# First layer of a two-layer cross-attention kernel: up projection as three fp32r products, keys and statistics at other positions

## The reference, cut to what matters

```python
q  = layer_norm(transpose(x   + pos_enc), ln_q_g,  ln_q_b)     # per batch: 512 tokens x 256 channels
kv = layer_norm(transpose(ctx + pos_enc), ln_kv_g, ln_kv_b)
Q, K, V = split(q @ Wq), split(kv @ Wk), split(kv @ Wv)         # 16 heads of 16
ctx = softmax(Q K^T / 4) V
r = ctx @ Wo + q
h = layer_norm(r, ffn_ln_g, ffn_ln_b)
h = gelu(h @ W1 + b1) @ W2 + b2                                 # 256 -> 512 -> 256
out = transpose(h + r)
```

## Time and profile before

| what | us |
|---|---|
| median of 3 runs | 1813.23 (1811.85 to 1816.99) |
| the profiled execution, its time | 1816.33 |
| its span, first to last instruction | 1814.5 |
| busy: PE, DVE, ACT, POOL | 1697.7, 1225.3, 1065.0, 166.1 |
| mean granted clock of TensorE | 0.96 |

### The profile page before, as it was taken

One profiled execution on the slowest core, in us unless ns is written; L12 is line 12 of the kernel. 1 busy time (PEld: TensorE's weight loads), 2 busy tenths in 40 slices (PEclk: granted clock), 3 DMA queues, 4 the chain that ended last, 5 costly groups with the idle time before them and its releaser, 6 DMA issues.

```text
span 1814.5 us, 32853 instructions
## 1 busy us (share of the span) xinstructions
PE 1697.7 (94%) x11968; PEld 1242.2 (68%) x11968; DVE 1225.3 (68%) x2812; ACT 1065.0 (59%) x2337; POOL 166.1 (9%) x221
## 2 busy tenths in 40 slices
PE   4779999999999998999999999999998799999999
PEld 3324444443534335788899888888887689999998
DVE  6667786867766653588888888888888653333332
ACT  3346666766666564587888777877778531111111
POOL 2102111010200000000000000000000100000000
PEclk7779999999999889999999999999999899999999
DMA  5322233222222224466567767666666330000000
GB/s 164 121 86 68 88 95 101 84 81 92 73 83 66 72 62 145 118 156 169 152 167 195 202 171 198 181 169 169 175 180 176 106 123 24 24 24 24 24 24 12
DMA packets 169481, 201.64 MB, mean 111 GB/s; under 512 B 25957, under 2 KB 117221, under 8 KB 169321
## 3 DMA queue, kind: packets, MB, share of 16 engines
q1 hardware_dynamic: 169032, 199.14, 38.8%
q10 hardware_dynamic: 288, 0.39, 0.1%
HBM read 131.84 MB, written 67.63 MB: 110 GB/s over the span
## 4 chain that ended last, share of the span: by engine, by line
PE 79%; DVE 12%; ACT 4%; issue 2%; DVEq 1%; DMA 0%; POOL 0%; ACTq 0%; SPq 0%
PE c_d L2230 10%; PE c_sums L2245 10%; PE b_d L1471 9%; PE b_d L1484 8%; PE a_d L531 5%; PE a_escore L504 5%; PE b_d L1551 5%; PE a_d L612 4%; PE a_d L620 3%; PE a_mscore L516 3%; DVE a_mx L870 3%; PE b_score L1539 3%; PE b_d L1568 3%; DVE b_t L1887 2%; DVE b_t L1883 2%
## 5 line engine op out<-in xcount | busy, mean ns | idle before, releaser
L870 DVE TENSOR_REDUCE a_mx<-a_mscore 128x2 f32<-128x1024 f32 x249 | 304.4, 1223 | 114.2 <-PE a_mscore L516 112.0
L689 ACT ACTIVATE a_pt<-a_escore 128x1024 f32<-128x1024 f32 x256 | 262.1, 1024 | 157.2 <-PE a_escore L504 156.6
L1709 ACT ACTIVATE b_pr<-b_t,b_nmax 128x256 f32<-128x256 f32 x512 | 254.5, 501 | 121.7 <-DVE b_nmax L1887 121.3
L2329 ACT ACTIVATE c_gT<-c_d,c_b 128x256 f32<-128x256 f32 x128 | 53.9, 473 | 266.9 <-PE c_d L2230 266.9
L1887 DVE CUSTOM_DVE_ANT_0 b_t<-b_t,b_minus 128x256 f32<-128x256 f32 x512 | 191.2, 429 | 16.9
L1883 DVE TENSOR_TENSOR b_t<-b_score,b_mask 128x1024 f32<-128x1024 f32 x128 | 155.1, 1212 | 64.3 <-PE b_score L1539 64.0
L2374 DVE CAST c_g_high<-c_gT 128x512 fp32r<-128x512 f32 x64 | 40.2, 627 | 172.0 <-ACT c_gT L2329 172.0
L504 PE MATMUL a_escore<-a_qst,a_kst 50*128 50x512 f32 x512 | 133.1, 516 | 18.4 <-ACT a_pt L689 16.8
L504 PEld LDWEIGHTS a_escore<-a_qst,a_kst 50*128 50x128 f32 x512 | 49.7, 191 | 143.7 <-ACT a_pt L689 87.8
L2230 PE MATMUL c_d<-c_ln_high,c_w_high 128*128 128x256 f32 x512 | 145.4, 284 | 2.4 <-DVE c_ln_low L2376 2.4
L2230 PE MATMUL c_d<-c_ln_low,c_w_high 128*128 128x256 f32 x512 | 145.6, 284 | 0.0
(11 more groups left out here) (175 smaller groups left out, 3301.2 us busy)
## 6 DMA issues: line engine op xcount, KB each, us to landing
b_qst<-b_q SPq DMA_DIRECT2D x96, 256.0 KB, 4.6
b_kst<-b_k SPq DMA_DIRECT2D x96, 256.0 KB, 6.4
b_q<-b_qparts SPq DMA_DIRECT2D x64, 256.0 KB, 4.0
b_k<-b_kparts SPq DMA_DIRECT2D x64, 256.0 KB, 3.5
a_qst<-a_q_parts SPq DMA_DIRECT2D x192, 64.0 KB, 2.2
a_kst<-a_k_parts SPq DMA_DIRECT2D x186, 64.0 KB, 2.2
a_q_parts<-a_qparts SPq DMA_DIRECT2D x32, 256.0 KB, 2.3
a_k_parts<-a_kparts SPq DMA_DIRECT2D x32, 256.0 KB, 2.4
```

The source lines that it names most:

```text
L689: nc.scalar.activation(pt[:, at % RING, :, :], escore[:], ACT.Exp, scale=SCALE).then_inc(exp_done.sem, 1)
L870: nc.vector.tensor_reduce(mx[:, 2 * pair:2 * pair + 2, q], maxima_bank(b, n)[:], AX_X, ALU.max).then_inc(max_done.sem, 1)
L1709: last = nc.scalar.activation(pr[:, u % 2, j, :], t[:, u % 2, j, :], ACT.Exp, scale=-1.0, bias=nmax[:, u, j:j + 1], accum_out=esum[:, u, j ...
```

## The change

The up projection `up` uses three fp32r products per step in place of one fp32 matmul. W1 gets a high and a low part (it is loaded to the staging area and split in iteration -1). Its input hT now lies in the third token tile, and its high and low parts (`high_hidden` on ScalarE, `low_hidden` on VectorE) in `pair`, the tile that also takes the parts of the context (`ctxp` before). The keys' second half moves from position 9 to 6 on all engines, the turn to channels of the network's input to slot 0 of position 5, both statistics of batch i+2 from positions 6 and 7 to 8 and their normalisations to 10 and 11 (but for iteration -2). The last quarter's `keep_up` moves to position 8.

```diff
@@ -129,7 +129,7 @@
         wo = sb("wo", [P, 2, CT, C], F32R)
-        w1 = sb("w1", [P, CT, F])
+        w1 = sb("w1", [P, 2, CT, F], F32R)
@@ -147,8 +147,7 @@
         ctxt = sb("ctxt", [P, TT, C])
-        ctxp = sb("ctxp", [P, 2, CT, T], F32R)
-        hT = sb("hT", [P, CT, T])
+        pair = sb("pair", [P, 2, CT, T], F32R)
@@ -168,20 +167,23 @@
-        kvn = tokn[1][:].rearrange("p (c t) n -> p c (t n)", c=CT)
+        kvn, hT = (tokn[s][:].rearrange("p (c t) n -> p c (t n)", c=CT) for s in (1, 2))
...
-            return pt[:, n].rearrange("p e t -> p (e t)")[:, 0:CT * C].rearrange("p (k n) -> p k n", k=CT)
+            columns = F if n == 3 else C
+            return pt[:, n].rearrange("p e t -> p (e t)")[:, 0:CT * columns].rearrange("p (k n) -> p k n", k=CT)
...
         late_in = sig("late_in", 1, 16)
-        w_high = sig("w_high", 3)
-        w_low = sig("w_low", 3)
+        w_high = sig("w_high", 4)
+        w_low = sig("w_low", 4)
+        h_high = sig("h_high", 1)
+        h_low = sig("h_low", 1)
@@ -236,11 +238,11 @@
             4: ["E0", "M0", ("pv", 0, 0, 0), ("pv", 0, 0, 1), "E1", "M1", ("pv", 0, 0, 2), ("pv", 0, 0, 3), ("m", 0, 2)],
-            5: ["E0", "M0", ("ctx", 0, 0), ("tok", 2, 1), "E1", "M1", ("chan", -1, 2)],
-            6: ["E0", "M0", ("f1", -1, 0, 0), ("f1", -1, 0, 1), "E1", "M1", ("f1", -1, 1, 0), ("f1", -1, 1, 1)],
-            7: ["E0", "M0", ("f1", -1, 2, 0), ("f1", -1, 2, 1), "E1", "M1", ("f1", -1, 3, 0), ("f1", -1, 3, 1)],
+            5: ["E0", "M0", ("chan", -1, 2), "E1", "M1", ("ctx", 0, 0), ("tok", 2, 1)],
+            6: ["E0", "M0", ("k", 1, 1, 0), ("k", 1, 1, 1), "E1", "M1", ("f1", -1, 0, 0), ("f1", -1, 0, 1)],
+            7: ["E0", "M0", ("f1", -1, 1, 0), ("f1", -1, 1, 1), ("f1", -1, 2, 0), "E1", "M1", ("f1", -1, 2, 1), ("f1", -1, 3, 0), ("f1", -1, 3, 1)],
             8: ["E0", "M0", ("pv", 0, 1, 0), ("pv", 0, 1, 1), "E1", "M1", ("pv", 0, 1, 2), ("pv", 0, 1, 3), ("m", 0, 3)],
-            9: [("k", 1, 1, 0), ("k", 1, 1, 1), ("q", 1, 1, 0), "E0", "M0", ("q", 1, 1, 1), ("ctx", 0, 1), "E1", "M1", ("f2", -1, 0, 0)],
+            9: [("q", 1, 1, 0), ("q", 1, 1, 1), "E0", "M0", ("ctx", 0, 1), "E1", "M1", ("f2", -1, 0, 0)],
@@ -368,7 +370,7 @@
                 load(qkv_in, dst, matrix(W[n]))
-            for dst, n in ((raw_weight(2), "Wo"), (w1[:], "W1"), (w2[:], "W2")):
+            for dst, n in ((raw_weight(2), "Wo"), (raw_weight(3), "W1"), (w2[:], "W2")):
@@ -554,7 +556,7 @@
                 for n, (x, y) in enumerate(PRODUCTS):
-                    mm = nc.tensor.matmul(at, wo[:, x, k, m * P:(m + 1) * P], ctxp[:, y, k, :],
+                    mm = nc.tensor.matmul(at, wo[:, x, k, m * P:(m + 1) * P], pair[:, y, k, :],
@@ -607,9 +609,13 @@
             def up(b, m, k):
-                pe_.wait_ge(chan_done[2].sem, chan_done[2].at(b, k + 1))
+                if b == 0 and m == 0 and k == 0:
+                    w_low.need(pe_, 0, 4)
+                pe_.wait_ge(h_low.sem, h_low.at(b, 1))
                 at = claim(pe_, "f1", b, m) if k == 0 else bank("f1", b, m)
-                mm = nc.tensor.matmul(at, w1[:, k, m * P:(m + 1) * P], hT[:, k, :], start=(k == 0), stop=(k == CT - 1))
+                for n, (x, y) in enumerate(PRODUCTS):
+                    mm = nc.tensor.matmul(at, w1[:, x, k, m * P:(m + 1) * P], pair[:, y, k, :],
+                                          start=(k == 0 and n == 0), stop=(k == CT - 1 and n == 2))
@@ -684,7 +690,7 @@
                 if b == 0 and n == 0:
-                    w_low.need(act, 0, 3)
+                    w_low.need(act, 0, 4)
@@ -708,16 +714,18 @@
                     return
-                y_filled.need(act, b - 1, CT)
+                f1_filled.need(act, b - 1, FT)
...
                     ctxT_filled.need(act, b, c + 1)
-                    nc.scalar.activation(ctxp[:, 0, c, :], bank("ctxT", b, c), ACT.Copy).then_inc(ctx_chan.sem, 1)
+                    nc.scalar.activation(pair[:, 0, c, :], bank("ctxT", b, c), ACT.Copy).then_inc(ctx_chan.sem, 1)
...
                     kvn_low.need(act, b - 1, 1)
+                elif s == 2:
+                    h_low.need(act, b - 1, 1)
@@ -736,13 +744,20 @@
                     dst = hT
-                    f1_filled.need(act, b - 1, FT)
+                    chan_filled[2].need(act, b, CT)
...
                                          bias=shifts[:, s, c:c + 1], scale=gains[:, s, c:c + 1]).then_inc(chan_done[s].sem, 1)
+            def high_hidden(b):
+                if not there(b):
+                    return
+                y_filled.need(act, b, CT)
+                chan_done[2].need(act, b, CT)
+                nc.scalar.activation(pair[:, 0], hT, ACT.Copy).then_inc(h_high.sem, 1)
@@ -786,11 +801,11 @@
             def high_weight(n):
-                if n == 2:
+                if n >= 2:
...
                     act.wait_ge(qkv_in.sem, 16 * QKV)
-                nc.scalar.activation((wk, wv, wo)[n][:, 0], raw_weight(n), ACT.Copy).then_inc(w_high.sem, 1)
+                nc.scalar.activation((wk, wv, wo, w1)[n][:, 0], raw_weight(n), ACT.Copy).then_inc(w_high.sem, 1)
@@ -803,17 +818,21 @@
                     high_weight(2)
+                    high_weight(3)
+                if p == 5:
+                    to_channels(i - 1, 2)
                 if p == 6:
+                    keep_tokens(i + 2, 1)
+                if p == 7:
                     keep_up(i - 1, 0)
-                if p == 7:
-                    keep_up(i - 1, 2)
                 if p == 8:
+                    keep_up(i - 1, 3)
...
                 if p == 9:
-                    high_part(i + 1, 1, 1)
+                    high_part(i + 1, 0, 1)
@@ -829,17 +848,15 @@
                 if p == 5:
-                    keep_tokens(i + 2, 1)
-                    to_channels(i - 1, 2)
+                    high_hidden(i - 1)
                 if p == 6:
+                    high_part(i + 1, 1, 1)
+                if p == 7:
                     keep_up(i - 1, 1)
-                if p == 7:
-                    keep_up(i - 1, 3)
+                    keep_up(i - 1, 2)
...
                     negative_maxima(i, 3)
-                if p == 9:
-                    high_part(i + 1, 0, 1)
@@ -903,7 +920,7 @@
             def low_weight(n):
-                w = (wk, wv, wo)[n]
+                w = (wk, wv, wo, w1)[n]
@@ -912,8 +929,14 @@
                     ctx_chan.need(dve, b, c + 1)
-                    nc.vector.tensor_tensor(ctxp[:, 1, c, :], bank("ctxT", b, c), ctxp[:, 0, c, :].bitcast(F32),
+                    nc.vector.tensor_tensor(pair[:, 1, c, :], bank("ctxT", b, c), pair[:, 0, c, :].bitcast(F32),
                                             ALU.subtract).then_inc(ctx_low.sem, 1)
+            def low_hidden(b):
+                if not there(b):
+                    return
+                h_high.need(dve, b, 1)
+                nc.vector.tensor_tensor(pair[:, 1], hT, pair[:, 0].bitcast(F32), ALU.subtract).then_inc(h_low.sem, 1)
@@ -969,14 +992,20 @@
                     normalise(i - 1, 2)
-                if p == 5:
-                    divide_context(i, 0)
                 if p == 6:
+                    low_hidden(i - 1)
+                    if i == FIRST:
+                        normalise(i + 2, 0)
+                        normalise(i + 2, 1)
+                if p == 7:
+                    low_part(i + 1, 1, 1)
+                if p == 8 and i != FIRST:
                     normalise(i + 2, 0)
-                if p == (6 if i == FIRST else 7):
...
                 if p == 9:
-                    low_part(i + 1, 1, 1)
+                    low_part(i + 1, 0, 1)
+                if p == 10 and i != FIRST:
+                    apply(i + 2, 0)
@@ -989,10 +1018,12 @@
                     low_maxima(i, 2)
-                if p == 6:
+                if p == 5:
+                    divide_context(i, 0)
+                if p == 6 and i == FIRST:
                     apply(i + 2, 0)
+                    apply(i + 2, 1)
                 if p == 7:
-                    apply(i + 2, 1)
@@ -1001,9 +1032,11 @@
                         low_weight(2)
+                        low_weight(3)
                 if p == 9:
-                    low_part(i + 1, 0, 1)
                     divide_context(i, 1)
+                if p == 11 and i != FIRST:
+                    apply(i + 2, 1)
```

## The result

The changed kernel takes **1839.54 us** (median, 1839.25 to 1841.83), beside 1812.63 us (1811.85 to 1816.99) for the kernel before: a ratio of 1.0146 [1.0128, 1.0165]. The forecast was 1834, range 1817 to 1850. The profiled execution's span went from 1814.5 to 1837.5 us, +23.0, against +21.0 in the forecast's sum.

The account below looks back on a forecast made before the run. TensorE bounds full slots, ScalarE positions 8 and 9. Opening 3.0, iterations 1 to 5 11.5, iteration 6 0.5, iterations 7 and 8 1, clock 5: +21.0 us, profiled 1837.3, median 1834; range 1817 to 1850.

Parts of the forecast that it names:

- the forecast's sum: Whole program: 3.0 + 0 + 11.5 + 0.5 + 1 + 5 = 21.0 us added to the profiled execution.
- the last step: From profiled execution (1837.3 us) to median: the profile stood 3.1 us above its median before, so 1834.
- The products' arithmetic: Up projection on TensorE: 0.22 us per matmul, 2.90 us for a slot of nine products, saving 1.4 us per batch.
- Rival (e): Up projection: fp32r products overlap more, a slot of six takes 1.7 us, total 1817 us; chance 0.02.
- Positions 5 to 7: Steady iteration: +0.2 us; the 1.4 us saving and ended hT wait are spent on 1.6 us of keys.
- Position 8: Statistics on VectorE delay the turn of maxima; TensorE stands 2.4 us, costing 2.1 us per steady iteration.
- The clock: Behind position 8's 2.4 us stand: a drop costs 1.3 us, 1.0 taken for each of 5 iterations, 5 us.
- The opening and iteration 0: Prologue: splitting delays the first turn of maxima from 56.49 to 59.4 us, +3.0 us; iteration 0 adds 0.
- iterations 7 and 8: Beside the second layer: 2.3 us of splitting ahead of the last up projection, which saves 1.4: +1 us.
- iteration 6: First layer iteration with no statistics left: 0.2 + 0.55 - 0.3, +0.5 us.
- the steady iterations: Iterations 1 to 5 of the first layer: +2.3 us each, 11.5 us.
- Rival (d): TensorE's work alone counts, 1803 us; decided by position 9's first scores coming within 7.6 us of position 8's; chance 0.09.

Follow-up runs that it names:

- Run 2: Changed kernel with the keys' second half back in position 9 on all engines: 1853.04 us, 1.0221.
- run 1: Changed kernel with both statistics behind, not ahead of, the second row maximum of position 8: 1828.56 us, 1.0083.
- run 7: Changed kernel with run 4's tail order, run 6's keep_up place, and the turn of maxima behind the query steps, statistics unmoved: 1819.16 us, 1.0032.
- run 4: Changed kernel with, in the tail, VectorE's positions 5 and 6 ahead of the second layer's statistics, normalisation and mask: 1832.66 us, 1.0107.
- run 8: Changed kernel with only the last quarter's keep_up back at the end of position 7: 1836.88 us, 1.0130.
- run 6: Run 5's kernel with the last quarter's keep_up back at the end of position 7: 1823.81 us, 1.0059.
- run 5: Changed kernel with the edits of run 1 and run 4 together: 1823.74 us, 1.0062.
- run 3: Changed kernel with statistics and their normalisations back at positions 6 and 7, as before the change: 1841.42 us, 1.0155.

## Why the prediction was right

It forecast slower, for the right reason, and the time within 5.5 us. Of these, 2.0 are the sum's (23.0 us of span, 21.0 forecast), and 3.5 come from the last step: it took the median to be 3.1 us below the profiled execution, as before, and after the change the two are 0.2 us apart. Step by step:

- **The products' arithmetic held.** Nine products, E and M: 2.97 us, forecast 2.90, so 0.23 us a matmul. Rival (e), and with it the sustained 131 ns of the Trainium skill, TensorE: Matmul & The Clock Gate, section Back-to-back issue gap, does not show here: the trace disagrees with it for these products.
- **Positions 5 to 7 held.** Forecast +0.2 us; by the exponentials +0.2 (4.90, 4.62, 5.98 us after, 5.33, 4.75, 5.20 before, means of iterations 1 to 5). As forecast, the saving is spent on the keys. Run 2 shows what the forecast did not see: without these keys the clock falls in position 6.
- **Position 8 held, a little oversized.** Stand 2.10 us, forecast 2.4; E(8,0) to E(9,0) 9.20, forecast 9.7. The row maximum ended 7.16 us after E(8,0), not 7.6; both statistics took 4.0 us, not 4.2. Per iteration +1.8 us, not +2.3. Runs 1 and 7 show the mechanism by removing it in two ways.
- **The clock was oversized.** 1.0 us in each of 5 iterations was taken; it was 1.4 and 1.2 in two and nothing in three, 2.6 in all. The price of one fall was right (1.3 forecast), how often was not. With the same stand run 4 had it in three and run 8 in all five. What decides it is open.
- **The opening and iteration 0: +3.0 forecast, +0.65 measured.** The first turn of maxima came at 58.33, not 59.4 (56.49 before). Iteration 0 gave 3.23 us back. Before, its granted clock is 0.50 in 100 to 110 and 0.83 in 110 to 120, after 0.98 and 0.68. The first exponential of batch 0 came between 70.3 and 73.8 in the ten variants, whose openings differ little. I read this stretch as carried by where the clock falls and not by a step of the program; that is argued, not shown.
- **The step that failed is "iterations 7 and 8": +1 forecast, +9.7 measured.** The prediction put it as "there ScalarE and VectorE add 2.3 us of splitting ahead of the last batch's up projection, which saves 1.4". It priced the subtraction by its duration and did not read what VectorE's stream has ahead of it in the tail. The low half was begun 3.8 us after its high half was ready, and TensorE stood 7.67 us. Run 4 took the queue away: the stand fell to 3.95 us, and 5.1 us came back between the turn to channels and the end of the up projection. On average over the kernels with and without that edit the end of the program gains 3.6 us. What is left of the stand is the chain of three steps itself, hT, high and low (in run 4 from 738.14 to 742.00), and the place takes 1.9 us longer than before even so (12.0, 10.2). The rest of the 9.7 us is spread over batch 7's exponentials and the second layer, and its cause stays open.

The tail was forecast 8.7 us too low and iteration 6 0.65; the clock 2.4, the steady iterations 2.7 and the opening with iteration 0 2.35 too high. That leaves the sum 2.0 us low of the span: an error of 9.35 us was offset by 7.4 us of errors the other way, so the close total is partly luck. Rival (d), faster, fell by the order of VectorE's stream, as was said against it. With that order mended (run 7) its condition is met, since E(9,0) comes after 7.41 us, and still the time is not 1803: by the exponentials positions 5 to 7 take 15.6 us there (15.3 before) and 8 and 9 take 10.8 (11.25), so the period is that of before, and nothing of the 1.4 us is left.

**Open:** the keys back in position 9 with run 7's order were not tried, so what they cost in position 6 once position 8 is mended is not known. Run 7's profile has the span of before (1814.4), but its median is 6.4 us above it. Iteration 6 (77.0 against 76.06) and the tail (1111.1 against 1110.1) account for 2. The profiled execution was the fastest of run 7's and near the top of the range of the kernel before, so the two profiles don't show the rest, and it was not found.

## What to carry to other kernels

Cheaper instructions on the bounding engine pay only if their new inputs come in time: write down the chain that makes each new operand, on every engine, and what each queue has ahead of it, in the steady loop and once more in the prologue and the tail, where another order holds. When work on a lesser engine must come late, look at what stands behind its consumer in the bounding engine's order; moving the consumer behind independent work (run 7, 1819.2 us) gave more than moving the producer (run 6, 1823.8 us, otherwise the same). And a step that looks like pure cost may be the filler that hides a latency and holds the clock: try taking it away before calling it one.

## What was not expected of the hardware

Two stands of 2.10 and 2.09 us at the same step, one iteration apart, differ in what follows: the clock stayed at 1.00 in one and fell in the other (query steps 1.94 and 3.12 us). In run 8, with the same stand, it fell in all five steady iterations (period 81.8 us). By a stand's length alone, at about 2.1 us, neither can be forecast; the price of such a fall here is 1.2 to 1.6 us.

Shorter stands did it too. In runs 1 and 5 TensorE does the same steps in positions 8 and 9 of iteration 2, with the same waits for ScalarE (0.78 us ahead of E(9,0), 0.35 ahead of E(9,1)). Behind them the first step of the down projection is, in run 1 and in run 5,

```profile
277.37 2.00 PE L626 MATMUL a_d<-a_gT,a_w 128*128 128x512 f32 x2
```

```profile
281.24 1.12 PE L626 MATMUL a_d<-a_gT,a_w 128*128 128x512 f32 x2
```

In run 1 that iteration takes 81.77 us, 3.0 more than iteration 1; in run 5 the clock falls in none of the five. In run 3 the waits there are 1.04 and 0.36 us, and it fell once in five iterations, for 3.3 us. What decides it was not found.
